# A spectral product whose VectorE half works in PSUM, small steps moved to GpSimd, a last output in halves, and new instruction orders

## Chip, cores and metric
The kernel runs on one core of one Trainium2 chip. The metric is the device time in microseconds of one execution; several executions give a median. Engines are called PE (TensorE), DVE (VectorE), ACT (ScalarE), POOL (GpSimd) and SP (SyncE).

## What is computed
Four batches of 512 tokens x 128 features pass through two layers; a context of 77 rows x 96 features is attended to. Cut to its outline:
```
x                                     # (4, 512, 128)
layer 0:
  scores of 4 heads over 77 context rows; only the 32 largest of a row are kept, softmax over these
  FiLM: scale and shift of the normed x from the attended context (film_in)
  s4d:  K from 64 complex states per feature; Kf = rfft(K), xf = rfft(z); y = irfft(xf * Kf); + D_skip
  FiLM again (film_out), norm, FFN with gelu, norm (norm 2), gated residual
  FFN whose two weights are butterfly products of 9 stages (512 wide)
layer 1:
  attention of 16 heads, 8 wide, over the 77 rows, gated residual
  mixture of 8 experts, rank 32, top 2: (silu(x Wu) * x Wv * gate) Wo, gated residual
```

## The kernel before, in words
Everything stays on chip: one batch is a tile of 128 partitions x 4 x 128. Each engine works through a hand-written list of steps, `ORDER` (lines 71 to 143): a step is a name and a batch, `mixr/0` for example, and an engine starts nothing of a later step before it has issued the earlier one. Between engines stand semaphores with constant values. `BANKS` (187 to 212) gives each PE step its PSUM banks, of which there are 8 of 128 x 512 floats; `readers` (399) says whose end makes a bank free. The steps of batch b + 1 are woven into those of batch b.

The steps that the change and the prediction touch:

- Attention of layer 0, for each batch and tile of 128 tokens: `score` (PE), four `round`s on DVE (line 1189: 4 times the 8 largest of a row, then replaced), `pick` (POOL, 1603), `wsum` and `winv` (DVE), `weigh` (POOL, 1608), `attnT` (PE). There are 64 rounds.
- Weight preparation: names that begin with `s_`. `s_ufly`, `s_udense`, `s_dfly`, `s_dhigh`, `s_dlow` (POOL) build the butterfly weights, `s_t1`, `s_wup`, `s_bup`, `s_t2`, `s_wdn`, `s_cwup` multiply them on PE, `s_pc`, `s_qc`, `s_kern`, `s_freq` give the spectrum of the state kernel, `s_misc` (DVE, 1470) scales two weights and fills two pads.
- The spectral part of a batch: `film_in` (PE, DVE 1234), `dft` on PE (two banks, even and odd tokens, 570), ACT copies the even bank to `XF` (942), DVE `dft` (1242) forms sum and difference with the odd bank, both in `XF`. Then `mixr` and `mixi` (DVE 1253, POOL 1617) multiply with `H0f` and `H1f`, the real and the imaginary part of the product, nine instructions each. DVE has `mixr` of batches 0, 1 and 3, POOL `mixr/2` and all four `mixi`. `idft` on PE waits for both. `film_pre` (PE, ACT, POOL 1556) prepares the second FiLM, `film_out` and `film_add` (DVE 1275) apply it, `stat1`, `rs1`, `norm1` and `lift1` follow.
- The first FFN: `ffn_up` (PE, ACT), `ffn_down` (PE, DVE 1285), then `stat2`, `rs2`, `norm2` (DVE, 1163), `gain` and `x1` (POOL), `stat3`, `norm3`, `lift3` and the second FFN, `fold_up` and `fold_down`.
- Attention of layer 1: `q`, `scoreA` (PE; DVE takes the maxima, 1172), `maxT` (DVE, 1177: the maximum as three bf16 terms in four dependent instructions; then PE, then ACT), `keyA`, `mixA`, `normA`, `wo`.
- The experts: `lift5`, `logits`, `top2` (DVE), `units` (PE, silu on ACT, product on DVE), `gate0` and `gate1` (POOL, 1573, two tiles each), `turn0` and `turn1` (four transposes each on PE, 678, a copy each on ACT), `moe_out` (PE; DVE adds, 1339). SP sends a batch's output (480) when it is added.

The elementwise helpers have one line each: L1118 is DVE's `tensor_tensor`, L1496 POOL's, L837 ACT's activation, L499 PE's matmul. `chain` issues an instruction and waits for it, `linked` only marks it. Setting up DMAs is SP's work alone. The code puts the two halves of the product so:
```
linked(tt(m0, x[:, :, 0, :, :], both(H0f[:, i, :, :]), ALU.mult))
chain(tt(m1, x[:, :, 1, :, :], both(H0f[:, 1 - i, :, :]), ALU.mult))
chain(tt(out, m0, m1, ALU.add if i else ALU.subtract))
```
where `x` is `XF` in SBUF.

## Time and profile before
| | us |
|---|---|
| median of 3 runs (334.46 to 335.09) | 334.61 |
| the profiled execution, its own time | 336.93 |
| its span, first to last instruction | 335.10 |
| PE busy in the span | 258.3 (77%) |
| DVE busy | 261.9 (78%) |
| ACT busy | 226.1 (67%) |
| POOL busy | 188.6 (56%) |

A profile is one execution, and its span lies inside its own time. Busy shares are means over stages that differ. The granted TensorE clock was 0.903 of full speed over the span. A row of a group gives its busy time, the mean of one instruction, and the idle time of the engine just before it with what ended it. A chain is followed back from the last instruction through what released each step.

### The profile page before, as it was taken

Reading aid. Unit: us, or ns where it says so; the run is one execution under the profiler, and the core shown is the slowest. Engines: PE = TensorE matmul, PEld = TensorE weight load, DVE = VectorE, ACT = ScalarE, POOL = GpSimd, SP = SyncE. Lnnn points to the kernel's source line nnn. Section 1 sums busy time; section 2 is a strip of 40 time slices with the busy share of each in tenths; the row PEclk is TensorE's granted clock in tenths of the full one; section 3 lists DMA queues with packets and bytes.
Section 4 is the critical chain, followed back from the end, with each engine's and each line's share of the span. In section 5 each row is a group of like instructions: output and inputs, shape, how many; then the busy total and the mean of one; then the engine's idle time right before and its main releaser. Section 6 shows DMA issues by size and latency. Waiting matters only on the chain.

```text
...
## 1 busy us (share of the span) xinstructions
PE 258.3 (77%) x1778; PEld 162.7 (49%) x1778; DVE 261.9 (78%) x1354; ACT 226.1 (67%) x534; POOL 188.6 (56%) x268
## 2 busy tenths in 40 slices
...
DMA packets 4663, 10.28 MB, mean 31 GB/s; under 512 B 659, under 2 KB 2836, under 8 KB 4374
## 3 DMA queue, kind: packets, MB, share of 16 engines
...
q8 instruction: 14, 0.23, 0.3%
...
## 4 chain that ended last, share of the span: by engine, by line
PE 47%; DVE 17%; POOL 15%; ACT 10%; issue 6%; POOLq 0%; ACTq 0%; DVEq 0%
PE bank L499 43%; ACT arena L837 5%; POOL arena L1496 5%; POOL MT L1496 4%; DVE arena L1118 4%; DVE R L1216 3%; DVE V L1204 2%; PE bank L521 2%; POOL k0bd L1496 1%; DVE KT L1447 1%; POOL bt L1496 1%; POOL sel L1606 1%; PE bank L683 1%; ACT E L837 1%; DVE st L1150 1%
## 5 line engine op out<-in xcount | busy, mean ns | idle before, releaser
L837 ACT ACTIVATE arena<-bank 128x512 f32<-128x512 f32 (+2 forms) x63 | 32.8, 597 | 21.2 <-PE bank L499 14.3
L1216 DVE MATCH_REPLACE8 R<-V,R 128x77 f32<-128x77 f32 x192 | 40.6, 223 | 0.0
L831 ACT ACT_TABLE_LOAD x29 | 37.2, 1283 | 4.2 <-DMA pack_kgen<-in_kgen 3.7
L1496 POOL TENSOR_TENSOR pack_bfly<-pack_bfly,bt 128x512 f32<-128x512 f32 x8 | 8.2, 1048 | 52.4 <-DVE bt L1118 42.7
L499 PE MATMUL bank<-arena 128*32 128x16 f32 (+3 forms) x304 | 13.2, 223 | 30.9 <-DVE arena L1118 29.6
L1204 DVE MAX8 V<-R 128x8 f32<-128x77 f32 x192 | 31.1, 224 | 0.4
L1174 DVE TENSOR_REDUCE bt<-bank 128x4 f32<-128x308 f32 x64 | 25.8, 468 | 5.8 <-PE bank L499 5.7
L499 PEld LDWEIGHTS bank<-arena 128*32 128x32 f32 (+1 forms) x304 | 9.9, 143 | 36.4 <-DVE arena L1118 31.2
L837 ACT ACTIVATE E<-bank,negm,rs 128x77 f32<-128x77 f32 x64 | 21.3, 415 | 7.3 <-POOL sel L1496 5.3
L499 PE MATMUL bank<-pack_bfly,arena 32*128 32x512 f32 (+3 forms) x136 | 21.0, 528 | 1.0 <-ACT pack_bfly L837 0.7
L1496 POOL TENSOR_TENSOR k0bd<-sel,w 128x308 f32<-128x308 f32 x16 | 11.6, 727 | 15.3 <-ACT w L837 15.0
L499 PE MATMUL bank<-pack_moe,LO 128*128 128x512 f32 (+1 forms) x64 | 19.6, 432 | 0.8 <-DVE bt L1174 0.5
L499 PE MATMUL bank<-LO,pack_ffn 128*128 128x512 f32 x32 | 17.8, 706 | 0.7 <-ACT LO L837 0.7
L499 PE MATMUL bank<-VW,AT 78*128 78x128 f32 x128 | 16.1, 279 | 2.4 <-ACT pack_dft L837 0.9
L1606 POOL TENSOR_SCALAR sel<-R 128x308 f32<-128x308 f32 x16 | 16.0, 1001 | 3.2 <-issue 2.2
L837 ACT ACTIVATE arena<-MT 128x128 f32<-128x128 f32 x74 | 17.3, 428 | 0.5 <-DVE MT L1118 0.5
L499 PEld LDWEIGHTS bank<-VW,AT 78*128 78x128 f32 x128 | 15.0, 192 | 4.3 <-ACT AT L837 2.0
L499 PE MATMUL bank<-arena,pack_dft 128*128 128x256 f32 x48 | 14.5, 447 | 2.5 <-DVE arena L1118 2.5
L1496 POOL TENSOR_TENSOR XG<-XG,pack_rows 128x512 f32<-128x512 f32 x4 | 5.1, 1272 | 18.9 <-DVE XG L1123 18.9
L499 PEld LDWEIGHTS bank<-pack_dft,arena 128*128 128x128 f32 x128 | 14.9, 192 | 1.1 <-issue 1.0
L1216 DVE MATCH_VALUE_LOAD R<-V,R 128x8 f32 x192 | 15.2, 79 | 0.4 <-POOL sel L1496 0.4
L499 PEld LDWEIGHTS bank<-pack_ffn,arena 128*128 128x128 f32 x128 | 14.9, 192 | 0.8 <-ACT arena L837 0.7
...
## 6 DMA issues: line engine op xcount, KB each, us to landing
...
```

The lines of the kernel that those rows point to most:

```text
L499: return nc.tensor.matmul(out, lhsT, rhs, start=start, stop=stop, **kw)
L521: last = nc.tensor.transpose(o[:, P * t:P * t + P], src[:, b, t, :], I)
L683: last = nc.tensor.transpose(o[:, P * t:P * t + P], SUT[:, t, P * tile:P * tile + P], I)
L831: nc.scalar.add_instruction(mybir.InstLoadActFuncSet(name=nc.get_next_instruction_name(), act_func_set_id=need, ins=[], outs=[]))
L837: return nc.scalar.activation(out, in_, func, **kw)
L1118: return nc.vector.tensor_tensor(out, x, y, op)
L1150: linked(nc.vector.bn_stats(st6[:, n, t, :], src[:, b, t, :]))
L1174: nc.vector.tensor_reduce(mx1[:, b % 2, tile, r, :], bank(f"sA{tile}_{r}", b)[:, 0:FLAT] .rearrange("p (h k) -> p h k", h=HG), AX.X, ALU.max)\
L1204: top = nc.vector.max(V8[:, g % 2, h, r, :], src[h])
L1216: swap = nc.vector.match_replace(R8[:, g % 2, r % 2, h, :], V8[:, g % 2, h, r, :], src[h], NEG)
L1496: return nc.gpsimd.tensor_tensor(out, x, y, op)
L1606: chain(nc.gpsimd.tensor_scalar(sel[:, g % 2, :, :], R8[:, g % 2, 1, :, :], -1.0e38, None, ALU.is_le))
```

## The change
- The spectral product: ACT copies the even bank to the second half of `XF`. DVE's `dft` forms sum and difference in four 256-wide instructions and writes them to the PSUM banks `d0` (real) and `d1` (imaginary) themselves. A new ACT step `xf` copies both banks to `XF` for POOL, in every batch. DVE's `mixr` works on the banks in PSUM, in nine instructions; POOL's halves read `XF` as before, in a new layout, and wait for the second copy.
- `maxT`'s split, `norm2` of all batches and `s_misc` go from DVE to POOL.
- Batch 3's experts: `gate0` on POOL takes tiles 0 and 1 one by one, `gate1` on DVE tiles 2 and 3. `turn0` transposes tiles 0 and 1 for both banks, `turn1` tiles 2 and 3. One copy is ACT's, the other DVE's. `moe_out` and a new `moe_rest` take half the tokens each, and each half has its own transfer; there are five output transfers for four.
- All four orders and the bank numbers are new.

The diff, cut; of the orders the lines of which the text speaks:
```diff
     "pe": """
...
-        score1/2 s_bup idft/0 score2/2 film_out/0 score3/2 vw/1 lift1/0 ffn_up0/0 ffn_up1/0 score0/3 s_t2
-        ffn_down/0 attnT/1 film_in/1 dft/1 s_cwup s_wdn film_pre/1 lift3/0 vw/2 vw/3 fold_up0/0 fold_up1/0
...
-        mixA1/3 mixA2/3 moe_out/1 wo/3 turn0/2 lift5/3 turn1/2 logits/3 units0/3 units1/3 units2/3 units3/3
-        moe_out/2 turn0/3 turn1/3 moe_out/3
...
+        s_bup vw/2 score2/2 idft/0 film_out/0 s_wup score3/2 s_cw1 lift1/0 ffn_up0/0 ffn_up1/0 s_t2 ffn_down/0
+        attnT/1 film_pre/1 score0/3 film_in/1 vw/3 s_cwup dft/1 score1/3 k1/0 s_wdn lift3/0 fold_up0/0
...
+        units2/1 units3/1 lift4/3 wo/2 q/3 turn0/1 scoreA0/3 turn1/1 scoreA1/3 scoreA2/3 scoreA3/3 lift5/2
+        moe_out/1 logits/2 maxT/3 keyA0/3 keyA1/3 mixA0/3 keyA2/3 mixA1/3 mixA2/3 units0/2 units1/2 units2/2
+        wo/3 units3/2 lift5/3 logits/3 turn0/2 turn1/2 units0/3 units1/3 units2/3 units3/3 moe_out/2 normA/3
+        turn0/3 turn1/3 moe_out/3 moe_rest/3
...
     "dve": """
...
-        film_in/0 round3_1/1 wsum0/1 round0_3/1 dft/0 winv0/1 round1_2/1 round1_3/1 wsum1/1 winv1/1 round2_2/1
-        stat0/3 round3_2/1 round2_3/1 round3_3/1 mixr/0 round0_0/2 round1_0/2 wsum2/1 round0_1/2 round2_0/2
-        round3_0/2 winv2/1 film_out/0 s_bup film_add/0 stat1/0 round0_2/2 wsum3/1 round1_1/2 round2_1/2
...
+        winv0/1 winv1/1 dft/0 nmr0/1 round0_0/2 s_freq mixr/0 round1_0/2 wsum2/1 round0_1/2 round2_0/2
+        round3_0/2 winv2/1 round1_1/2 wsum3/1 round0_2/2 film_out/0 film_add/0 round2_1/2 stat1/0 wsum0/2
...
+        stat5/3 top2/3 units0/3 units1/3 units2/3 units3/3 gate1/3 moe_out/2 turn1/3 moe_out/3 moe_rest/3
     "pool": """
...
-        s_ufly2 s_ufly3 weigh1/0 pick3/0 s_ufly4 weigh2/0 weigh3/0 s_ufly5 s_ufly6 s_ufly7 pick0/1 s_ufly8
-        s_udense pick1/1 mixi/0 weigh0/1 pick2/1 s_dfly2 s_dfly3 s_dfly4 s_dfly5 weigh1/1 pick3/1 film_pre/0
...
+        s_ufly1 s_ufly2 s_dfly2 s_ufly3 s_ufly4 s_dfly3 s_dfly4 weigh2/0 weigh3/0 pick0/1 pick1/1 s_ufly5
+        s_ufly6 s_ufly7 s_ufly8 s_udense s_rows film_pre/0 weigh0/1 weigh1/1 pick2/1 mixi/0 pick3/1 weigh2/1
...
+        s_dfly5 pick0/2 s_dfly6 s_dfly7 s_dfly8 s_dhigh weigh3/1 pick1/2 x_bias/0 weigh0/2 pick2/2 norm2/0
+        gain/0 x1/0 s_dlow film_pre/1 weigh1/2 mixi/1 pick3/2 s_v1 weigh2/2 weigh3/2 x_bias/1 pick0/3 s_misc
+        pick1/3 k1/0 norm2/1 gain/1 x1/1 mixi/2 maxT/0 mixr/2 film_pre/2 k1/1 k1/2 weigh0/3 x_bias/2 pick2/3
...
+        def mixed(b, i):
+return [(s["dft_moved"], 3 * b + i)] + [made("mixr", b)] * (("mixr", b) in SCHEDULE["dve"])
...
-for b in range(B):
+for b in range(B - 1):
     sp.wait_ge(s["x4_ready"], b + 1)
     sp.dma_start(tokens(out_dram[b]), by_parity(X[:, b, :, :])).then_inc(stored, 16)
-sp.wait_ge(stored, 16 * B)
+for c in range(2):
+    sp.wait_ge(s["x4_ready"], B + c)
+    sp.dma_start(tokens(out_dram[B - 1])[:, c], by_parity(X[:, B - 1, :, :])[:, c]).then_inc(stored, 16)
+sp.wait_ge(stored, 16 * (B + 1))
...
+    elif step.startswith("turn") and b == B - 1:
+        if tile == 0:
+            pe.wait_ge(s["weighted"], 2 * b + 1)
+            claim("turn0", b)
+            claim("turn1", b)
+        else:
+            pe.wait_ge(s["gated"], NT * B + 1)
+        for j in range(2):
+            for t in (2 * tile, 2 * tile + 1):
+                last = nc.tensor.transpose(bank(f"turn{j}", b)[:, P * t:P * t + P], SUT[:, t, P * j:P * j + P], I)
+            if tile == 1:
+                last.then_inc(s["turn_ready"], 1)
     elif step.startswith("turn"):
...
+    elif step in ("moe_out", "moe_rest"):
+        o = claim("moe" if step == "moe_out" else "moe_rest", b)
         pe.wait_ge(s["turned"], 2 * b + 2)
-        for t in range(NT):
+        for t in (range(NT) if b < B - 1 else range(0, 2) if step == "moe_out" else range(2, NT)):
...
-        a(XF[:, 0, :, :, :].rearrange("p s c d -> p (s c d)"), bank("d0", b)[:, :], ACT.Copy).then_inc(s["dft_moved"], 1)
+        a(flat4(XF[:, 1, :, :, :]), bank("d0", b)[:, :], ACT.Copy).then_inc(s["dft_moved"], 1)
+    elif step == "xf":
+        for i in range(2):
+            act.wait_ge(s["dft_copied"], 4 * b + 2 * i + 2)
+            a(flat4(XF[:, i, :, :, :]), bank(f"d{i}", b)[:, :], ACT.Copy).then_inc(s["dft_moved"], 1)
...
-        dve.wait_ge(s["dft_moved"], b + 1)
-        low, high = (XF[:, f, :, :, :].rearrange("p s c d -> p (s c d)") for f in range(2))
-        tt(high, low, bank("d1", b)[:, :], ALU.subtract).then_inc(s["dft_copied"], 1)
-        tt(low, low, bank("d1", b)[:, :], ALU.add).then_inc(s["dft_copied"], 1)
+        dve.wait_ge(s["dft_moved"], 3 * b + 1)
+        even, odd = flat4(XF[:, 1, :, :, :]), bank("d1", b)
+        for i in range(2):
+            x, y, o = even[:, CH * i:CH * i + CH], odd[:, CH * i:CH * i + CH], bank(f"d{i}", b)
+            if i == 1:
+                dve.wait_ge(s["dft_copied"], 4 * b + 2)
+            tt(o[:, 0:CH], x, y, ALU.add).then_inc(s["dft_copied"], 1)
+            tt(o[:, CH:2 * CH], x, y, ALU.subtract).then_inc(s["dft_copied"], 1)
     elif step == "s_freq":
...
-    elif step in ("mixr", "mixi"):
-        dve.wait_ge(s["dft_copied"], 2 * b + 2)
+    elif step == "mixr":
+        dve.wait_ge(s["dft_copied"], 4 * b + 4)
         if b == 0:
             dve.wait_ge(s["freq_copied"], 3)
         if b >= 1:
             dve.wait_ge(s["y_ready"], b)
-        i, x = int(step == "mixi"), XF
+        re, im = (bank(f"d{i}", b)[:, :].rearrange("p (f c d) -> p f c d", f=2, c=2) for i in range(2))
         both = lambda t: t.unsqueeze(2).broadcast_to([P, 2, 2, D])
-        out = YZ[:, i, :, :, :]
-        m0, m1 = (MT[:, 2 * i + k, :, :].rearrange("p f (c d) -> p f c d", c=2) for k in range(2))
-        linked(tt(m0, x[:, :, 0, :, :], both(H0f[:, i, :, :]), ALU.mult))
-        chain(tt(m1, x[:, :, 1, :, :], both(H0f[:, 1 - i, :, :]), ALU.mult))
-        chain(tt(out, m0, m1, ALU.add if i else ALU.subtract))
-        linked(tt(m0[:, :, 0, :], x[:, :, i, 0, :], H1f[:, 1, :, :], ALU.mult))
-        chain(tt(m1[:, :, 0, :], x[:, :, 1 - i, 0, :], H1f[:, 0, :, :], ALU.mult))
-        chain(tt(out[:, :, 1, :], out[:, :, 1, :], m0[:, :, 0, :], ALU.add))
-        chain(tt(out[:, :, 1, :], out[:, :, 1, :], m1[:, :, 0, :], ALU.subtract if i else ALU.add))
-        low, high = (YZ[:, i, f, :, :].rearrange("p c d -> p (c d)") for f in range(2))
-        even, odd = halves(i)
+        out = YZ[:, 0, :, :, :]
+        k0, k1 = (MT[:, 0, k, :].rearrange("p (f d) -> p f d", f=2) for k in range(2))
+        m1 = MT[:, 1, :, :].rearrange("p f (c d) -> p f c d", c=2)
+        dve.wait_ge(s["dft_moved"], 3 * b + 2)
+        chain(tt(k0, re[:, :, 0, :], H1f[:, 1, :, :], ALU.mult))
+        linked(tt(re, re, both(H0f[:, 0, :, :]), ALU.mult))
+        dve.wait_ge(s["dft_moved"], 3 * b + 3)
+        linked(tt(k1, im[:, :, 0, :], H1f[:, 0, :, :], ALU.mult))
+        chain(tt(m1, im, both(H0f[:, 1, :, :]), ALU.mult))
+        chain(tt(re[:, :, 1, :], re[:, :, 1, :], k0, ALU.add))
+        chain(tt(re[:, :, 1, :], re[:, :, 1, :], k1, ALU.add))
+        chain(tt(out, re, m1, ALU.subtract))
+        low, high = (YZ[:, 0, f, :, :].rearrange("p c d -> p (c d)") for f in range(2))
+        even, odd = halves(0)
         tt(even, low, high, ALU.add)
...
+    elif step == "gate1":
+        dve.wait_ge(s["gated"], NT * b + NT)
+        dve.wait_ge(s["gate_ready"], b + 1)
+        x = SUT[:, 2:4, :].rearrange("p t (e r) -> p t e r", e=NE)
+        tt(x, x, W8[:, b % 2, 2:4, :].unsqueeze(3).broadcast_to([P, 2, NE, RE]), ALU.mult).then_inc(s["gated"], 1)
+    elif step == "turn1":
+        dve.wait_ge(s["turn_ready"], 2 * b + 2)
+        dve.wait_ge(s["moe_ready"], 2 + b)
+        nc.vector.tensor_copy(SU[:, 1, :], bank("turn1", b)[:, :]).then_inc(s["turned"], 1)
+    elif step in ("moe_out", "moe_rest") and b == B - 1:
+        half = int(step == "moe_rest")
+        dve.wait_ge(s["moe_ready"], 2 + b + 1 + half)
+        x, part2 = X[:, b, 2 * half:2 * half + 2, :], slice(256 * half, 256 * half + 256)
+        tt(flat(x), bank("moe_rest" if half else "moe", b)[:, part2], flat(x), ALU.add).then_inc(s["x4_ready"], 1)
...
+    elif step == "maxT":
+        hi, mid, lo = (MXS[:, :, :, HG * i:HG * i + HG] for i in range(SPLIT))
+        pool.wait_ge(s["maxed"], RG * NT * (b + 1))
+        if b == 0:
+            linked(nc.gpsimd.memset(MXS[:, :, :, :], 0.0))
+            pool.wait_ge(s["pool_link"], link[0])
+        if b >= 1:
+            pool.wait_ge(s["maxT_ready"], b)
+        chain(nc.gpsimd.tensor_copy(hi, mx1[:, b % 2, :, :, :]))
+        chain(tt(mxr[:, :, :, :], mx1[:, b % 2, :, :, :], hi, ALU.subtract))
+        chain(nc.gpsimd.tensor_copy(mid, mxr[:, :, :, :]))
+        tt(lo, mxr[:, :, :, :], mid, ALU.subtract).then_inc(s["split_ready"], 1)
...
+    elif step.startswith("gate") and b == B - 1:
+        pool.wait_ge(s["gate_ready"], b + 1)
+        for i in range(2):
+            pool.wait_ge(s["gated"], NT * b + i + 1)
+            x = SUT[:, i, :].rearrange("p (e r) -> p e r", e=NE)
+            last = tt(x, x, W8[:, b % 2, i, :].unsqueeze(2).broadcast_to([P, NE, RE]), ALU.mult)
+        last.then_inc(s["weighted"], 1)
...
-        pool.wait_ge(s["dft_copied"], 2 * b + 2)
+        pool.wait_ge(s["dft_moved"], 3 * b + 3)
```

## Rows read from the trace of the kernel before

**Rows 1.** Stretch, length; busy us of PE, PEld, DVE, ACT, POOL; clock; DMA share
```profile
20.00:110.00 90.00, 42.35 (x431) 30.56 (x432) 86.61 (x530) 58.86 (x174) 81.15 (x130) 0.70 0.07 25
...
145.00:327.20 182.20, 175.62 (x1157) 104.56 (x1155) 126.95 (x576) 130.56 (x267) 72.48 (x89) 1.00 0.01 4
327.20:335.10 7.90, 3.12 (x24) 2.72 (x24) 1.38 (x2) 1.08 (x2) 0.61 (x1) 1.00 0.19 66
```

**Rows 2.** Stretches again, of instructions on tile MT alone (DVE's spectral products)
```profile
93.20:99.40 6.20, 0.00 (x0) 0.00 (x0) 5.50 (x8) 0.00 (x0) 0.00 (x0) 0.70 0.00 0
147.50:152.40 4.90, 0.00 (x0) 0.00 (x0) 4.41 (x8) 0.00 (x0) 0.00 (x0) 1.00 0.02 5
232.20:237.30 5.10, 0.00 (x0) 0.00 (x0) 4.54 (x8) 0.00 (x0) 0.00 (x0) 1.00 0.00 2
```

**Rows 3.** DVE instructions on tile MT: min/median/max ns, first and last start
```profile
L1118 DVE TENSOR_TENSOR MT<-arena,pack_film x6: 677/930/1227, 93.2 to 233.3; 128x512 f32<-128x512 f32 x6
```

**Rows 4.** Groups by form on DVE: busy us, mean ns, idle before
```profile
L1118 DVE TENSOR_TENSOR pack_bfly<-bank,pack_bfly 128x256 f32<-128x256 f32 x16 | 5.9, 418 | 1.5 <-ACT pack_bfly L837 1.5
...
L1118 DVE TENSOR_TENSOR arena<-arena,bank 128x512 f32<-128x512 f32 x8 | 5.1, 675 | 0.8 <-PE bank L499 0.8
...
L1118 DVE TENSOR_TENSOR XG<-HN,XG 128x512 f32<-128x512 f32 x4 | 2.8, 690 | 0.1
```

**Rows 5.** Groups by form on ACT
```profile
L837 ACT ACTIVATE arena<-bank 128x512 f32<-128x512 f32 x45 | 23.9, 610 | 14.9 <-PE bank L499 8.1 <-PE bank L683 6.7
```

**Rows 6.** Groups by form on POOL
```profile
L1496 POOL TENSOR_TENSOR bt<-pack_bfly,v 128x64 f32<-128x64 f32 x6 | 3.0, 521 | 0.2
...
L1553 POOL TENSOR_SCALAR HN<-X,rs 128x128 f32<-128x128 f32 x4 | 2.3, 603 | 17.8 <-ACT rs L837 17.8
...
L1496 POOL TENSOR_TENSOR bt<-pack_bfly,bflyh 128x64 f32<-128x64 f32 x6 | 1.9, 336 | 0.2
```

**Rows 7.** Groups by form on DVE: norm 2, and two of the split's four
```profile
L1123 DVE TENSOR_SCALAR XG<-XG,mv,rs 128x128 f32<-128x128 f32 x16 | 5.0, 373 | 0.3 <-ACT rs L837 0.3
...
L1118 DVE TENSOR_TENSOR pack_bfly<-pack_bfly 128x64 bf16<-128x64 f32 x4 | 1.5, 368 | 0.1
...
L1186 DVE CAST pack_bfly<-bt 128x64 bf16<-128x64 f32 x4 | 0.9, 229 | 0.1
```

**Rows 8.** The chain that ended last, in order of time: start us, us, what
```profile
40.02 0.56 DVE V L1204 x4
40.58 0.83 DVE R L1216 x4
...
114.70 6.71 PE bank L499 x8
```

**Rows 9.** Timeline: start us, us, instruction, in brackets the idle time before it
```profile
84.96 1.27 POOL L1496 TENSOR_TENSOR MT<-arena,pack_film 128x512 f32<-128x512 f32 x1
...
103.04 1.43 PE L499 MATMUL bank<-MT,pack_dft 128*128 128x256 f32 x4
...
108.82 0.69 DVE L1118 TENSOR_TENSOR HN<-bank,AO 128x512 f32<-128x512 f32 x1 [1.72 <-POOL XG L1496]
```

**Rows 10.** Timeline of PE, the two waits for DVE's maxima
```profile
295.15 0.63 PE L683 MATMUL bank<-pack_first,pack_bfly 128*128 128x128 f32 x4 [0.71 <-DVE bt L1174]
...
301.04 1.95 PE L499 MATMUL bank<-pack_moe,LO 128*128 128x512 f32 x4 [0.54 <-DVE bt L1174]
```

**Rows 11.** Timeline of the tail
```profile
325.76 2.05 POOL L1496 TENSOR_TENSOR pack_bfly<-pack_bfly,bt 128x512 f32<-128x512 f32 x2 [8.98 <-DVE pack_bfly L1118]
...
329.79 2.02 PE L499 MATMUL bank<-pack_moe,arena 128*128 128x128 f32 x16 [0.83 <-ACT arena L837]
331.85 0.69 DVE L1118 TENSOR_TENSOR X<-bank,X 128x512 f32<-128x512 f32 x1 [3.93 <-PE bank L499]
```

**Rows 12.** Timeline of POOL, the first step of two weighs
```profile
93.34 1.15 POOL L1496 TENSOR_TENSOR k0bd<-sel,w 128x308 f32<-128x308 f32 x1
...
103.86 0.70 POOL L1496 TENSOR_TENSOR k0bd<-sel,w 128x308 f32<-128x308 f32 x1
```

194 lines of the change are left out of this document (88 added, 106 removed).

## The prediction
> **What bounds the kernel now.** I read the busy time by stretch first, then the chain of waits, then groups and single rows. The stretches [rows 1] show two regimes. From 20 to 110 us VectorE (DVE) is busy 86.6 of 90 us and GpSimd (POOL) 81.2, while TensorE (PE) has 42.4 and runs at a mean granted clock of 0.70 (1.0 is 2.4 GHz, 0.5 is 1.2): attention's top-32 rounds and the weight preparation set the pace. From 145 to 327.2 us PE is busy 175.6 of 182.2 us at full clock, so only 6.6 us there are PE's idle time, and DVE has 55 us free. Between them lies a ramp, and after 327.2 a serial tail of 7.9 us with 3.1 us of matmuls. So time can come from four places: an earlier end of the first regime, PE work placed ahead of the ramp's end, PE's 6.6 us, and the tail. A share of busy time on DVE after 145 is worth nothing by itself.
>
> The profiled execution took 336.93 us around a span of 335.10; the median of the runs is 334.61, 2.3 below it. I make the sum as a difference against that execution and take it off the median.
>
> **Part by part.**
>
> *Spectral product.* DVE runs three of these (b = 0, 1, 3; `mixr/2` is GpSimd's). Eight of the nine instructions took 5.50, 4.41 and 4.54 us [rows 2]; with the ninth (a 256-wide one, 0.45) a product is 5.3 on average. The dear ones read two SBUF operands: 677 ns at best, 1227 at worst for the same 512 columns [rows 3]. New: three 512-wide at the price of a form with one PSUM input, 0.68, and six 256-wide at 0.42 [rows 4], together 4.6. That saves 0.7 three times. `dft` becomes four 256-wide (1.68) for two 512-wide (1.35), 0.3 dearer four times. DVE nets 0.9 us. No row shows DVE writing PSUM: for 512 columns the ends are 0.60 (the ACT row that reads a bank [rows 5], less for a write that doesn't leave PSUM) and 0.93 (the median of the SBUF form), and I take 0.68, the row whose read side is the same; the ends are 3 x 3 x -0.08 = -0.7 us and 3 x 3 x 0.25 = +2.2. ScalarE (ACT) gets two more copies of 0.61 [rows 5] in each of four batches, 4.9 us, hidden by its 52 idle us in the PE-bound stretch. For GpSimd they are latency: it starts after the second copy, about 1.0 us later than the old pair of 0.675.
>
> The rows give 512 columns 0.68 with a PSUM input and 0.69 with two SBUF inputs [rows 4]. The Trainium skill, page "VectorE: DVE Perf Modes", section on the TRN2 errata, charges 120 cycles a VectorE instruction from PSUM against 58 from SBUF. By that rule, an estimate from the page, three products (27 instructions of 65 ns more) would be about 1.7 us dearer, wiping out the gain, and the median 332.7, inside the first case's spread. This trace doesn't show such a difference, so the sum goes by the rows.
>
> *Norm 2 to GpSimd.* DVE loses 5.0 us [rows 7]. The nearest GpSimd row is 0.60 for 128 columns with one scalar [rows 6], 2.4 us a batch; with two scalars perhaps up to 1.0 each, 4.0. I take 2.4. Latency per batch is +1.0 against DVE's 1.25, and at b = 0 DVE no longer does `film_in/1` first, so it is even there. Behind it wait `gain` and `x1` of the same queue.
>
> *Maxima's split.* On DVE four instructions between 0.23 and 0.37 [rows 7], about 1.3 us a batch; on GpSimd 64-column rows are 0.34 to 0.52 [rows 6], so 1.6 to 2.4. I take 1.9: 0.6 later into `maxT`, with PE steps (fold_down or logits) put before it. At b = 0 it stands between `mixi/2` and `mixr/2`, and its wait for the last maximum blocks the latter. `s_misc`: 0.9 us off DVE, about 1.6 on, in a GpSimd queue that has room then.
>
> *First regime.* A round is 0.56 + 0.83 us plus its joints, 1.45 [rows 8]. Ahead of DVE's `film_out/0` the new order has two more rounds (2.9), `wsum3/1` (0.5) and the dearer `dft/0` (0.3), less `mixr/0`'s 1.4 (6.0 there) and 0.4 of small steps: 1.9 more. But `film_out/0` waited 1.72 for GpSimd's `film_pre/0` [rows 9], which now runs before `mixi/0`. So it starts at 109.0 instead of 108.8. Ahead of `mixi/0` GpSimd gets s_dfly2 to 4 (3.7), `film_pre/0` (1.3), two weighs (2.9) and a pick (1.8), 9.7 us, less some 3 us of waits it had: 85.0 + 6.7 = 91.7, at the latest 97. It ends 8.4 later (84.96 to the next step's 93.34 before [rows 9, 12]) at 100 to 105.4; idft takes 3.1, so y is there at 103.2 to 108.5, under DVE's 109.0. The old idft started at 103.0 [rows 9], behind s_wup and s_bup on PE. By `ffn_down/0` DVE's work ahead is equal (0.2 apart), and `ffn_up`, 6.7 us of PE at the low clock, sets it [rows 8]. I take 0, from -3 (full clock there, no DVE waits) to +3.
>
> *Ramp.* Ahead of `fold_up0/0` PE has now also done score1/3 (0.8) and k1/0 (0.3): -1.1. Film_pre/1 now precedes mixi/1, so film_out/1 no longer waits 0.4: -0.4.
>
> *PE-bound stretch.* PE's work is unchanged. Of its 6.6 idle us, DVE's maxima made 1.25 in two waits [rows 10]; DVE has 11.5 us less before the tail. But scoreA1 to A3 of b = 3 now stand together, so PE will wait for maxima there (6.5 of DVE for 3.2 of PE), repaid by lift5/2, moe_out/1 and logits/2 covering the split. I take -1.0, from -4 to +3.
>
> *Tail.* Before [rows 11]: GpSimd's two gates to 327.81, transposes to 328.96, two ACT copies, then 2.02 of matmuls from 329.79, add 0.69, transfer. New: DVE gates tiles 2 and 3 while GpSimd does 0 and 1, ready about 327.2, when PE ends `moe_out/2`. Transposes to 328.4, copies on ACT and DVE side by side to 329.1, matmuls to 331.1, the last add 0.42 to 331.6 against 332.54. The first half's transfer is under it. -1.0, and 0.1 for half the bytes: -1.1. A DMA issue more on the otherwise empty SP queue costs nothing on the path.
>
> Sum: 0 - 1.1 - 0.4 - 1.0 - 1.1 = -3.6, so 336.93 becomes 333.3 for that execution, and the median 331.0.
>
> **Rivals.**
> *The first regime really shortens* (0.20). DVE's work up to the end of attention is about 4.3 us less (two norms, the first split, the products); if its waits also go and PE finds full clock earlier, the ramp starts 3 to 4 sooner: 331.0 - 3.5 = 327.5. For: DVE's 96% before 110. Against: at `ffn_down/0` the work ahead hasn't changed.
> *GpSimd becomes the bound* (0.24), the slow side. Its place is `mixi/0`: 9.7 us pulled ahead of it on an engine already busy 90% [rows 1]. It decides once mixi/0 ends after about 106. With contended prices (that stretch has 1.15 for a weigh's first step against 0.70 [rows 12]) and 3 us waiting for the last pick it ends at 109.5, y at 112.6, 3.6 late; norm 2 at its upper price adds 1.6 at b = 0, the split 0.5. The later gains are then worth 2.5 less the 1.0 that DVE no longer frees: 334.6 + 3.6 + 1.6 + 0.5 - 3.5 = about 336.8.
> *Only the tail counts* (0.14). The PE-bound stretch absorbs the rest: 334.61 - 1.1 = 333.5, or 334.4 if one of the new joints costs 1.0.
> The forecast's own case has 0.42, spread 329 to 333.
>
> **Numbers.** About 0.2% (0.67 us) is what a measurement can tell from no change. Faster: 0.42 + 0.20 + a little under half of 0.14 = 0.68; same 0.08; slower 0.24. The range takes in 327.5 less 1.7 and the slow case's 336.8: 325.8 to 336.8.
>
> **What would show it.** Right: `film_out/0` without a wait for GpSimd near 109; DVE's product instructions at 0.68 and 0.42, with no spread, DVE busy some 250 us and GpSimd 204; `fold_up0/0` within 1 us of 145; PE idle 5 to 6 us from there to moe_out/2; from the last GpSimd gate to the end 7 us. Wrong: DVE's `film_out/0` or PE's idft waiting for GpSimd by over 2 us, 128-column norms of 1 us on GpSimd, PSUM-writing instructions above 0.8, PE idle above 9 us after the ramp, or the low clock lasting beyond 145.

## The result, and the profile of the changed kernel

The changed kernel takes 341.46 us, the median of three runs (340.56 to 349.93); the kernel before 334.61. The ratio is 1.0172, with a 95% interval from 1.0144 to 1.0201: slower by 5.8 us by the ratio, where I had forecast 331.0. Two later sets of runs, on other chips, gave 1.0174 (1.0033 to 1.0315) and 1.0136 (1.0091 to 1.0180), 5.8 and 4.6 us. Kernels here fall at times into a slower state, of which the 349.93 is one execution; ratios, intervals and spans leave such executions out, and where the profiled one was of them (the changed kernel's first, its second repetition, "norm 2 back", "product back") nothing rests on TensorE's time in it alone. What follows is read from a second profile of the changed kernel, 339.78 us around a span of 338.0.

The busy time by stretch of that execution (columns as in [rows 1]):

```profile
20.00:110.00 90.00, 40.01 (x425) 29.72 (x426) 88.87 (x550) 54.29 (x170) 78.06 (x130) 0.70 0.08 28
110.00:145.00 35.00, 30.61 (x164) 21.11 (x164) 32.12 (x190) 26.77 (x64) 30.88 (x43) 1.00 0.01 2
145.00:331.60 186.60, 177.28 (x1148) 105.49 (x1147) 117.24 (x542) 129.49 (x264) 87.46 (x121) 0.98 0.01 4
331.60:338.00 6.40, 2.93 (x25) 2.53 (x23) 2.23 (x4) 0.60 (x1) 0.00 (x0) 1.00 0.23 82
```

The ramp (second row) has its full clock now, and the tail (fourth) is 6.4 us where it was 7.9 [rows 1]. But the PE-bound stretch went from 182.2 to 186.6 us: PE's idle time in it grew from 6.6 to 9.3, and its busy time by 1.7, though the matmuls are the same and nearly 4 us of them now stand before 145 (`fold_up0/0` starts 2.6 us earlier, with 1.1 us of steps put ahead of it). Its mean granted clock is no longer full (0.98; 1.0 is 2.4 GHz, 0.5 is 1.2). PE's timeline shows the place (start us, us, instruction, in brackets the idle time before it and what ended it):

```profile
174.44 1.36 PE L507 MATMUL bank<-arena,pack_bfly 32*128 32x308 f32 x8
178.12 1.18 PE L507 MATMUL bank<-arena,pack_bfly 32*128 32x308 f32 x8 [2.33 <-DVE bt L1200]
179.24 0.82 PE L529 MATMUL bank<-pack_first,HN 128*128 128x128 f32 x4
179.99 3.73 PE L507 MATMUL bank<-arena,pack_bfly 32*128 32x308 f32 x16
183.65 5.06 PE L507 MATMUL bank<-LO,pack_dft 128*128 128x512 f32 x8
```

These are `scoreA0/0`, `scoreA1/0`, `lift3/1`, `scoreA2/0` with `scoreA3/0`, and `fold_up` of batch 1. (A matmul in f32 stands as two instructions, so x8 is four matmuls, and `fold_up0/1` is the first half of the last row.) PE waits for DVE's maxima, and then `fold_up0/1` takes 3.35 us instead of 1.98. In the kernel before PE came to these steps later, did not wait, and ran all of `fold_up` in 3.70 us:

```profile
177.01 2.47 PE L499 MATMUL bank<-arena,pack_bfly 32*128 32x308 f32 x16
182.74 3.70 PE L499 MATMUL bank<-LO,pack_dft 128*128 128x512 f32 x8
178.07 1.40 DVE L1174 TENSOR_REDUCE bt<-bank 128x4 f32<-128x308 f32 x3
```

The same stretch of the changed kernel by windows, with the clock in the third column from the end:

```profile
174.00:178.00 4.00, 1.79 (x13) 0.91 (x11) 2.52 (x13) 2.69 (x8) 3.92 (x4) 1.00 0.00 0
178.00:181.00 3.00, 2.88 (x20) 2.04 (x23) 2.09 (x6) 1.71 (x5) 2.84 (x4) 0.77 0.00 0
181.00:188.00 7.00, 7.00 (x22) 3.24 (x15) 6.59 (x36) 2.42 (x4) 5.94 (x12) 0.61 0.01 2
```

Four microseconds with PE busy 1.79, then ten at a mean clock of 0.66, so 6.8 of them at 1.2 GHz.

The orders differ too much to compare step by step. So I put every matmul to its step (by count, against the order list), took for each kind of step the shortest time it has in any trace, and compared the moments at which equally much of this work was left. In us against the profiled execution of the kernel before (minus is ahead):

```
work left, near       changed  tail   norm 2   product  two-matmul  norm+round  norm+banks+round
                               alone  alone    alone    filler      (t11)       (t7)
175  ffn_down/0        -2.5    -0.6    -1.4     -0.6      -2.2       -2.7        -2.2
135  film_pre/2        -2.4    -0.7    +0.4     +1.1      -1.4       -2.7        -1.4
125  keyA1/0           +2.3    -0.7    +5.3     +2.6      +0.6       -2.1        -1.4
 90  lift3/2           +3.3    -0.7    +7.3     +4.3      +1.6       -0.4        +0.4
 70  logits/0          +2.0    -0.7    +6.9     +3.5      +0.3       -2.4        -1.7
 50  mixA0/2           +4.4    -0.7    +7.0     +3.5      +2.7       +3.2        +0.8
  5  units3/3          +4.4    -0.6   +10.2     +1.7      +2.7       +4.5        +0.4
  0  moe_out/3         +2.7    -2.4   +10.2     +1.7      +1.0       +2.7        -1.3
```

The change is 2.5 us ahead at the end of the first regime, loses 4.7 within 10 us of work at the first batch's maximum scores, 2.4 more in batch 2 (between 70 and 50), and gains 1.7 in the tail. From its first row to the one before the last it goes from -2.5 to +4.4. The execution compared is among the changed kernel's better ones: its spans are 337.8 to 341.9 us, at granted clocks of 0.87 to 0.91, where the kernel before has 0.90 to 0.91 in most of its runs. And the profiled execution of before is 1.4 to 2.3 us above the medians of its sets (336.93 against 335.54 and 334.61). So the two profiles differ by 2.9 us, where the medians of the second repetition differ by 5, and the table shows only part of the loss.

### The profile page after: what moved, and what is told of

Read it like the earlier page. It is cut to its first block, busy times and chain, and to the rows that moved or that the text cites. A ratio compares the mean times of both kernels' runs of the same rounds, so it can differ in the third digit from the quotient of the medians.

```text
span 348.1 us, 6239 instructions
## 1 busy us (share of the span) xinstructions
PE 272.4 (78%) x1778; PEld 171.2 (49%) x1778; DVE 255.2 (73%) x1328; ACT 226.8 (65%) x539; POOL 203.1 (58%) x305
## 4 chain that ended last, share of the span: by engine, by line
PE 46%; DVE 14%; ACT 5%; POOL 5%; issue 2%; POOLq 0%; DVEq 0%; ACTq 0%
PE bank L507 43%; DVE R L1229 4%; ACT arena L858 3%; DVE V L1217 3%; POOL XG L1575 2%; DVE bt L1200 2%; PE bank L529 1%; DVE bank L1144 1%; DVE arena L1144 1%; ACT pack_bfly L858 1%; DVE MT L1144 1%; DVE st L1176 1%; ACT LO L858 1%; POOL X L1521 1%; POOL XG L1521 1%
## 5 line engine op out<-in xcount | busy, mean ns | idle before, releaser
L858 ACT ACTIVATE arena<-bank 128x512 f32<-128x512 f32 (+2 forms) x70 | 36.6, 600 | 15.5 <-PE bank L507 10.1
L507 PE MATMUL bank<-arena 128*32 128x16 f32 (+3 forms) x304 | 17.1, 239 | 9.0 <-DVE arena L1144 6.9
L507 PE MATMUL bank<-arena,pack_bfly 32*128 32x308 f32 x128 | 19.5, 523 | 4.9 <-DVE bt L1200 4.1
L1521 POOL TENSOR_TENSOR pack_bfly<-pack_bfly,bt 128x512 f32<-128x512 f32 (+1 forms) x8 | 7.5, 940 | 23.6 <-DVE pack_bfly L1144 23.6
L507 PEld LDWEIGHTS bank<-arena 128*32 128x32 f32 (+1 forms) x304 | 13.4, 165 | 15.0 <-issue 7.6
L1144 DVE TENSOR_TENSOR X<-bank,X 128x512 f32<-128x512 f32 (+1 forms) x13 | 8.4, 646 | 15.5 <-PE bank L507 15.4
L1144 DVE TENSOR_TENSOR pack_bfly<-bank,pack_bfly 128x256 f32<-128x256 f32 (+1 forms) x20 | 9.0, 476 | 14.6 <-ACT pack_bfly L858 14.6
L858 ACT ACTIVATE LO<-bank 128x512 f32<-128x512 f32 x16 | 9.5, 598 | 15.5 <-PE bank L529 15.4
L507 PE MATMUL bank<-LO,pack_dft 128*128 128x512 f32 x32 | 17.0, 676 | 1.4 <-ACT LO L858 1.4
L1575 POOL TENSOR_SCALAR XG<-XG,mv,rs 128x128 f32<-128x128 f32 x16 | 12.5, 793 | 8.9 <-ACT rs L858 8.8
```

The lines of the kernel that those rows point to most:

```text
L507: return nc.tensor.matmul(out, lhsT, rhs, start=start, stop=stop, **kw)
L858: return nc.scalar.activation(out, in_, func, **kw)
L1144: return nc.vector.tensor_tensor(out, x, y, op)
L1521: return nc.gpsimd.tensor_tensor(out, x, y, op)
L1575: last = nc.gpsimd.tensor_scalar(dst[:, b, t, :], src[:, b, t, :], mv[:, tile, b, t, 0:1], rs[:, tile, b, t:t + 1], ALU.subtract, ALU.mult)
```

## The experiments

*The changed kernel again.* First, once more alone; then on the chip of the next three kernels.

> The changed kernel once more, unchanged, because its first profiled run was a disturbed one. Theory 1 (the clock: TensorE has less work in small pieces before 50 us, stands for 2 to 4 us at some new joints and then runs the next tens of matmuls at 1.2 GHz, late in the kernel too) expects 341 us within 1, a mean granted clock of 0.88 to 0.89 against 0.903 before, VectorE, ScalarE and GpSimd no busier than in the kernel before, and at least two stretches at the low clock behind 145 us that the kernel before does not have. Theory 2 (the GpSimd queue became the bound) expects the clock after 145 us to be full as before, and the idle time of TensorE to grow by 6 us or more, put down to GpSimd. Theory 3 (the first regime only ends later) expects fold_up of the first batch to start at 150 us or later instead of 145, and everything behind it as far apart as before.

> The changed kernel unchanged, on the chip of the next three, so that they can be set against it on one chip: 340 to 342 us, ratio to before 1.015 to 1.02.

339.78 us at best, clock 0.909 in the profile; GpSimd's work after 145 has grown (87.5 us for 72.5), but of PE's waits after 142 none is put down to it. Theory 3 falls: `fold_up0/0` starts at 142.40. Theory 1 has the mechanism, but not its size: one stretch at the low clock behind 145 in this profile, not two. The 6.8 us at half clock are worth at most 3.4 us of work, and PE's idle time has grown by 2.7, so both count, and about equally. Theory 2 falls by its own test, though not in substance, as the DVE row below shows. The second set: 340.56.

*Other banks.*
```diff
- scoreA1/0:7350 lift3/1:1 scoreA2/0:6573 scoreA3/0:0145
+ scoreA1/0:6451 lift3/1:0 scoreA2/0:7346 scoreA3/0:5170
```
(left out: other banks for `fold_up` of batch 1 too, and 1 and 5 exchanged from `fold_down/1` on)

> The changed kernel with other PSUM banks for the four maximum-score steps of the first batch (scoreA1 to A3) and what follows them; no order and no instruction is changed. Theory A (the loss sits where the scores for the row maxima stand: scoreA1/0's first bank is one whose maximum VectorE takes third, so TensorE waits 2.33 us and then runs the next 7 us of matmuls at the low clock) expects scoreA1/0 to start within 0.3 us of scoreA0/0's end, fold_up of batch 1 to start 2 to 3 us earlier and to take 1.98 instead of 3.35 us, and the undisturbed executions 3 to 4 us shorter, 336 to 337 us against 339.8. Theory B (VectorE's sixteen maxima, 6.5 us, set that place whatever the banks) expects less than 1 us. Theory C (the loss comes from the parts moved to GpSimd) expects nothing, within 0.3 us.

Ratio 1.0277 (1.0239 to 1.0316), slower than the changed kernel. `scoreA1/0` started at once, and the wait came back one and two steps later; PE began `fold_up0/1` at 183.25, 0.4 us earlier than in the changed kernel, and at the low clock (whole, the last row is 6.15 us for x8):

```profile
175.56 2.32 PE L507 MATMUL bank<-arena,pack_bfly 32*128 32x308 f32 x14
178.47 0.78 PE L507 MATMUL bank<-arena,pack_bfly 32*128 32x308 f32 x2 [0.59 <-DVE bt L1200]
179.98 0.66 PE L529 MATMUL bank<-pack_first,HN 128*128 128x128 f32 x4 [0.73 <-DVE bt L1200]
180.57 2.75 PE L507 MATMUL bank<-arena,pack_bfly 32*128 32x308 f32 x16
183.25 4.64 PE L507 MATMUL bank<-LO,pack_dft 128*128 128x512 f32 x5
```

So these banks are not the bound at this place (theory A falls, B stands for it): sixteen maxima of 0.47 us are, from the moment DVE can start them. That the whole is some 4 us slower than the changed kernel, no theory expected.

*The parts alone, in the old orders.* The tail:
```diff
- units3/3 moe_out/2 moe_out/3
+ units3/3 gate1/3 moe_out/2 turn1/3 moe_out/3 moe_rest/3
```
(left out: the code of gates, transposes, and halves of the sum and of the output)

> The kernel before, its orders and banks untouched, with the tail part of the change alone: the last batch's gates on both engines, its second copy of the transposes on VectorE, the last product, sum and output in halves. My prediction's price was 1.1 us; the changed kernel's undisturbed trace has 6.4 us from the end of moe_out/2 to the end of the span, where the kernel before had 7.9. Theory A expects 1.1 to 1.5 us less than the kernel before, 335.4 to 335.8 for an execution like the profiled one of before (336.93). If the saving needs the new orders around it, 0.5 or less.

333.73 us against 335.51, ratio 0.9949 (0.9929 to 0.9969): by its interval the only kernel of all that beats the one before, and so the version to keep. The table gives it 1.7 us between 5 us before the end and the end.

All small moves (norm 2, the split, the small set-up step), and norm 2 alone, which in outline is:
```diff
- norm2/b (VectorE)     gain/b (GpSimd)
+                       norm2/b gain/b (GpSimd)
```

> The kernel before with the small moves alone, in the old orders: norm 2 of every batch, the maxima's split and the small set-up step go from VectorE to GpSimd, at the nearest place in its queue. Theory A (the new orders and banks lose the time, not the moves) expects within 1 us of the kernel before either way. Theory C (GpSimd's slower norm, 3.1 us a batch against 1.1 on VectorE, and a split of 1.6 ahead of maxT are on the path) expects 2 to 5 us more, with TensorE waiting for GpSimd at fold_up or maxT of several batches.

> The kernel before with norm 2 alone moved to GpSimd, directly ahead of gain in its queue; nothing else. With all small moves the old orders lost some 14 us. If the norm is the cause (3.13 us a batch against 1.11 on VectorE, all of it ahead of gain, x1 and stat3), batch 0 loses about 2 us at fold_up0/0 and batch 1 about 2 at the maximum scores, and with the low clock behind such waits it is 4 to 12 us. If the maxima's split is the cause, this run is within 2 us of before.

Ratios 1.0446 (1.0374 to 1.0518) and 1.0332 (1.0304 to 1.0360). Theory A was wrong about the moves, C right in sign and far too low (all of them cost 15 us): norm 2 alone costs 11 here. Its price (group by form, in the changed kernel's profile; columns as in [rows 6, 7]):

```profile
L1575 POOL TENSOR_SCALAR XG<-XG,mv,rs 128x128 f32<-128x128 f32 x16 | 12.5, 795 | 7.0 <-ACT rs L858 6.9
```

and the place, PE in the kernel before with norm 2 alone on GpSimd:

```profile
177.41 1.58 PE L498 MATMUL bank<-arena,pack_bfly 32*128 32x308 f32 x12
179.71 0.89 PE L498 MATMUL bank<-arena,pack_bfly 32*128 32x308 f32 x4 [0.72 <-DVE bt L1173]
...
182.27 3.36 PE L498 MATMUL bank<-arena,pack_bfly 32*128 32x308 f32 x16
185.56 6.21 PE L498 MATMUL bank<-LO,pack_dft 128*128 128x512 f32 x8
```

It is the place of the changed kernel, and again the clock falls behind it: `fold_up` takes 6.21 us for 3.70. Two more losses follow, in the maximum scores of batch 1 (+2.0) and the key scores of batch 3 (+3).

The product alone (old orders, the copies added, `scoreA3/1` put ahead of `units2/0`, banks chosen anew), and the reverse, the changed kernel with the product back in SBUF:
```diff
-                "d1": [(s["dft_copied"], 2 * b + 2)], "y": [(s["y_scaled"], b + 1)],
+                "down": [(x_ready["v"], b + 1)], "d0": mixed(b, 2), "d1": mixed(b, 3), "y": [(s["y_scaled"], b + 1)],
...
+                elif step == "xf":
```
(left out: the copies themselves; the two banks `d0` and `d1` are free only when ScalarE's copies and `mixr` are done)

> The kernel before with the spectral product's part alone (VectorE's half in PSUM, four butterflies, ScalarE's two extra copies), the old orders but for the new copies and one pair of TensorE steps swapped, and banks chosen anew for the longer hold of dft's two banks. VectorE saves 0.3 us a product less the dearer butterflies; the two banks are held 15 to 20 us in batches 0 and 3, in batch 3 through the maximum scores of batch 1, where nine banks would be wanted. Theory D (bank pressure) expects 2 to 4 us lost between 222 and 230 us and about that in all; my prediction's terms alone expect within 1 us of before.

> The changed kernel with the spectral product put back as it was (VectorE reads and writes SBUF, two butterflies, one ScalarE copy per batch instead of three), in the new orders and with the new banks. Theory A expects the wait at scoreA1/0 to stay, because its banks are the same, and the time within 1 us of the changed kernel. Theory D (the product in PSUM itself costs: two banks held until ScalarE's two extra copies are done, the copies ahead of film_pre's) expects 1.5 to 4 us less than the changed kernel, with the waits behind dft of each batch gone.

1.0116 (1.0080 to 1.0153) and 1.0594 (1.0522 to 1.0666). Alone the product costs 3.9 us by the ratio and 2.0 between the two profiled executions. That is theory D's sum, but only a part of it lies at the place D had named (222 to 230 us): 1.2 to 1.3 at `fold_down/0` to `idft/1`, 1.5 at batch 0's maximum scores and 1.1 around `units` of batch 0, where PE's `scoreA3/1` takes 1.88 us for 0.80 and `units3/0` waits 0.92. At the maximum scores the clock falls here too:

```profile
182.00:186.00 4.00, 4.00 (x22) 2.29 (x23) 2.13 (x7) 1.89 (x3) 3.77 (x5) 0.57 0.00 0
```

How much of the cost is the held banks, and how much the two extra copies or the new bank numbers elsewhere, no run separates. Taking it out of the new orders, though, costs some 15 us (1.0594 against 1.014 to 1.017), which no theory expected. DVE's instructions on the product's tile in that kernel (min/median/max ns, first and last start):

```profile
L1134 DVE TENSOR_TENSOR MT<-arena,pack_film x6: 680/767/1754, 93.2 to 245.1; 128x512 f32<-128x512 f32 x6
L1134 DVE TENSOR_TENSOR MT<-arena,pack_kgen x6: 837/1159/1487, 95.7 to 248.8; 128x256 f32<-128x256 f32 x6
```

the second of these groups in the kernel before, where GpSimd's half ran at another time:

```profile
L1118 DVE TENSOR_TENSOR MT<-arena,pack_kgen x6: 416/424/653, 95.9 to 235.1; 128x256 f32<-128x256 f32 x6
```

and the same multiplications in PSUM, in the changed kernel:

```profile
L1144 DVE TENSOR_TENSOR MT<-bank,pack_kgen x6: 410/414/424, 93.7 to 234.6; 128x256 f32<-128x256 f32 x6
L1144 DVE TENSOR_TENSOR bank<-bank,MT x6: 432/432/433, 95.8 to 236.1; 128x256 f32<-128x256 f32 x6
L1144 DVE TENSOR_TENSOR bank<-bank,pack_film x3: 699/699/699, 94.1 to 234.0; 128x512 f32<-128x512 f32 x3
```

The new orders run `mixr/0` (93.7 to 99.7) beside GpSimd's `mixi/0` (95.5 to 104.1); the old ones had them one behind the other [rows 2, 9, 12]. With SBUF operands and GpSimd beside it a 256-column multiplication takes 837 to 1487 ns, with an operand in PSUM at most 424; `mixr/0` takes 9.3 us against 6.0. So the product in PSUM is what makes the overlap of the two engines cheap. How the 15 us come out of that was not followed step by step.

*Norm 2 back on VectorE, in the new orders*, in outline:
```diff
- (GpSimd) norm2/b gain/b
+ (GpSimd) gain/b   (VectorE) round3_3/2 norm2/0 · film_in/2 norm2/1 · scoreA2/1 norm2/2 · wo/1 norm2/3
```

> The changed kernel with norm 2 of all four batches back on VectorE and nothing else. Theory N (the norm on GpSimd costs 3.13 us a batch where VectorE took 1.1, and in batches 0 and 1 all of it is latency of the chain norm 2, gain, x1, stat3: VectorE waits 1.68 and 1.48 us for x1 just before stat3) expects stat3 1.5 to 2 us earlier in batch 0 and 0.7 to 1 in batch 1, fold_up of batch 0 to start near 140.5 instead of 142.4, and 2 to 4 us less in all, 336 to 338. Theory B (VectorE's queue ahead of the sixteen maxima sets the pace, and the norm only fills it again) expects fold_up0/0 earlier but scoreA3/0 where it was, and less than 1 us in all. A loss of more than 1 us would say that VectorE is the bound there.

Inconclusive by its time: one execution of four counts, 339.16. But `fold_up0/0` was no earlier in it (142.79, against 142.40), and in t11 and t7 below, which have norm 2 back too, it starts at 142.19 and 142.74: at batch 0 ScalarE gets to the copy of `lift3/0` only at 142.1 (t7), behind the product's two extra copies, `s_cwup` and `k1/0`. Here theory N is wrong.

*Useless work in the wait.* Four, then two matmuls of `fold_up`'s shape behind `scoreA0/0`, into a free bank that nobody reads:
```diff
- scoreA0/0 scoreA1/0
+ scoreA0/0 spare/0 scoreA1/0
```

> The changed kernel with four useless matmuls of 512 columns (about 2 us at the full clock) behind scoreA0/0, in the 2.33 us in which TensorE waits for VectorE's maxima; they write a free PSUM bank that nobody reads. Theory C (the wait costs twice: itself, and then 6.8 us of the low clock over fold_up of batch 1) expects the clock to stay full there, fold_up0/1 to take 1.98 instead of 3.35 us, and the undisturbed executions 1.5 to 3.5 us shorter although work was added. Without that mechanism: the same time as the changed kernel, or up to 0.5 us more.

> The changed kernel with two useless matmuls of 512 columns behind scoreA0/0; one takes about 0.95 us, so they fill 1.9 of the 2.33 us for which TensorE waits there. If the low clock behind the wait is worth what the trace says (fold_up0/1 3.35 instead of 1.98 us, and some 0.4 us in the small steps), the clock stays full to the end and the time is 1.5 to 2 us below the changed kernel's, 338 to 338.7, with 3 us of the 5 lost at this place left. If the clock falls anyway, 340 as without.

Four took 3.63 us, not the 2 I had reckoned, and gave 1.0130 (1.0088 to 1.0171); two gave 1.0102 (1.0039 to 1.0165), a median of 338.06 us where the changed kernel had 340.56 on another chip. The intervals of both overlap the changed kernel's (1.0091 to 1.0180), so the whole time doesn't tell; the trace does, at this place. PE with the two, and its windows:

```profile
176.76 1.98 PE L507 MATMUL bank<-LO,pack_ffn 128*128 128x512 f32 x4
179.16 1.18 PE L507 MATMUL bank<-arena,pack_bfly 32*128 32x308 f32 x8 [0.42 <-DVE bt L1204]
...
180.86 2.56 PE L507 MATMUL bank<-arena,pack_bfly 32*128 32x308 f32 x16
183.35 2.84 PE L507 MATMUL bank<-LO,pack_dft 128*128 128x512 f32 x6
```

```profile
175.00:178.00 3.00, 3.00 (x16) 1.63 (x16) 1.53 (x11) 1.76 (x4) 2.92 (x4) 1.00 0.00 0
178.00:181.00 3.00, 2.58 (x15) 1.16 (x14) 2.51 (x7) 1.82 (x7) 2.84 (x4) 1.00 0.00 0
181.00:188.00 7.00, 6.95 (x34) 3.80 (x35) 6.94 (x35) 4.80 (x7) 6.47 (x12) 1.00 0.01 2
```

(Whole, the last row of the timeline is 3.70 us for x8.) Full clock over the place, and a loss of 2.0 us there (-1.4 to +0.6) instead of 4.7. Both PE and DVE come to it 1.03 us later in this execution (scores from 175.47, maxima from 177.89), whose clock was low from 143.7 to 147.1, so the two losses start from the same distance between the engines. So more than half of what the wait costs here is the clock behind it: nothing but useless work was added. The Trainium skill, page "TensorE: Matmul & The Clock Gate", section "What's actually happening", has this rule (the array's clock halves after idleness, and the same kernel may meet it differently from run to run). The traces agree with both: the clock fell behind the wait and not behind the filled one, and executions of the one changed kernel have mean clocks from 0.87 to 0.91. A fall that no wait explains comes below, in t11.

*Which edits carry the repair.* All three (t7: norm 2 back, other banks, one top-32 round from before to behind the maxima), then without the banks (t11), then without norm 2 (t12). The round's edit:
```diff
- film_in/2 norm2/1 round2_2/3 dft/2 ... scoreA3/0 round0_3/3
+ film_in/2 norm2/1 dft/2 ... scoreA3/0 round2_2/3 round0_3/3
```

> Norm 2 back on VectorE, the renamed banks of the earlier run, and one top-32 round (1.47 us) moved from before to behind the first batch's sixteen maxima on VectorE. Theory B (VectorE's place for the maxima is what TensorE waits for) expects scoreA0/0 on VectorE at 174.5 to 175.5 instead of 176.9, TensorE without a wait over 0.5 us among the maximum scores, fold_up0/1 begun by 181 at the full clock, and 4 to 6 us less than the changed kernel, 334 to 336. If the clock falls anyway, 2 us less.

> The changed kernel with norm 2 on VectorE and the one top-32 round behind the sixteen maxima, its PSUM banks as they are. If VectorE's start of the maxima carries the gain (they start 1 us or more earlier against the scores), the time is 335 to 337, with scoreA1/0's wait at most 1.3 instead of 2.33 us. If the banks are needed too, 338 to 341 and the low clock still follows the wait.

> The changed kernel with the renamed banks and the one round behind the maxima, norm 2 still on GpSimd. VectorE then stands 3 us before stat3/1, waiting for x1 behind GpSimd's norm, so the maxima can't start earlier: if norm 2's latency is the cause, the time stays at 340 to 344 and GpSimd's x1/1 is what stat3/1 waits for. If it isn't, 335 to 337 as with all three.

In this order the ratios are 1.0003 (0.9980 to 1.0026), 1.0270 (1.0189 to 1.0351) and 1.0254 (1.0214 to 1.0294). DVE before the maxima in the changed kernel:

```profile
172.76 1.56 DVE L1144 TENSOR_TENSOR bank<-arena,bank 128x256 f32<-128x256 f32 x4 [0.69 <-PE bank L507]
175.79 0.87 DVE L1176 BATCH_NORM_STATS2 st<-X 128x6 f32<-128x128 f32 x4 [1.48 <-POOL X L1521]
```

GpSimd in front of it:

```profile
169.92 3.13 POOL L1575 TENSOR_SCALAR XG<-XG,mv,rs 128x128 f32<-128x128 f32 x4 [0.81 <-ACT rs L858]
173.13 1.28 POOL L1521 TENSOR_TENSOR XG<-XG,pack_rows 128x512 f32<-128x512 f32 x1
174.49 1.27 POOL L1521 TENSOR_TENSOR X<-XG,X 128x512 f32<-128x512 f32 x1
```

and without norm 2 back, the round moved (t12): the wait is still there, so the maxima can't start earlier; with it back (t7) it is gone:

```profile
177.48 0.87 DVE L1175 BATCH_NORM_STATS2 st<-X 128x6 f32<-128x128 f32 x4 [1.47 <-POOL X L1520]
```
```profile
175.46 0.87 DVE L1173 BATCH_NORM_STATS2 st<-X 128x6 f32<-128x128 f32 x4
176.52 2.76 DVE L1197 TENSOR_REDUCE bt<-bank 128x4 f32<-128x308 f32 x7
```

(In t7 the maxima start at 176.52, not at 174.5 to 175.5 as expected, because PE's scores themselves came 1.0 us later, and PE waited 0.93 for ScalarE's norm before `lift3/1`.) Norm 2 with the round is what repairs this place: t11, with the old banks, passes it at -2.1 (table). Its maxima start at 175.19 instead of 176.86, and its PE waits 0.97 us instead of 2.33, with `fold_up` at the full clock:

```profile
176.47 1.18 PE L504 MATMUL bank<-arena,pack_bfly 32*128 32x308 f32 x8 [0.97 <-DVE bt L1197]
```

Whether norm 2 back would do there without the round, no run decides. That t11 is nonetheless no faster than the changed kernel is a second matter: its clock fell at 268 and again at 302 us, and t7's did not, though from 190 us on the two differ in the numbers of two banks only. The windows of t11, then those of t7 0.7 us later, at the same steps:

```profile
266.00:269.00 3.00, 2.87 (x24) 1.61 (x20) 2.02 (x4) 2.92 (x6) 1.91 (x2) 0.88 0.00 0
269.00:276.00 7.00, 7.00 (x37) 1.76 (x33) 2.58 (x18) 2.42 (x6) 0.00 (x0) 0.57 0.00 1
```
```profile
266.70:269.70 3.00, 2.87 (x28) 1.42 (x21) 1.99 (x4) 2.95 (x7) 1.94 (x2) 1.00 0.00 0
269.70:276.70 7.00, 7.00 (x65) 2.16 (x57) 2.79 (x20) 3.69 (x10) 0.00 (x0) 1.00 0.00 1
```

What decides it is open: PE is as busy in both just before, and has the same waits, so this fall isn't that of the place at 179 us, where PE had stood. t11's three spans are 338.0 to 341.2 us, t7's seven 332.9 to 334.6, so without the banks the repair of the place brings nothing in the whole, and why the banks matter is not shown.

*All remaining waits at once*, by orders and banks, on top of t7 (t8; left out here: `lift5/2` among batch 3's maximum scores, `mixr/1` one round later, the banks from batch 2's key scores on):
```diff
- scoreA1/0 lift3/1 scoreA2/0     idft/1 film_out/1 score2/3     keyA1/2 logits/1 keyA2/2 mixA0/2     norm3/0 xf/1 s_cwup k1/0 lift3/0
+ scoreA1/0 scoreA2/0 lift3/1     score2/3 idft/1 film_out/1     keyA1/2 mixA0/2 logits/1 keyA2/2     norm3/0 s_cwup lift3/0 xf/1 k1/0
```

> The kernel of the last run (norm 2 on VectorE, renamed banks, one round behind the maxima) with its remaining waits taken on, by orders and banks alone: in batch 0 ScalarE copies lift3 before the product's two extra copies; scoreA2/0 stands ahead of lift3/1; one text score stands ahead of idft/1; in batch 2 mixA0 stands between the key scores, and lift5/2 among batch 3's maximum scores. Theory B (what is lost behind the ramp are places where TensorE is ahead and finds a bank, a copy or a maximum not ready) expects fold_up0/0's wait 0.7 instead of 1.4 us, 0.5 us less at scoreA of batch 0, 0.5 to 1 less in batch 2 and 0.5 in batch 3: 332.5 to 334 where the last had 335.6. If it is 335 or more, the waits only move on.

335.56 us, ratio 1.0010 (0.9984 to 1.0036): a miss. Each wait it took away came back a step later (0.7 us won at `fold_up0/0`, 1.04 lost at `idft/1`, which then stood behind the later copies; 1.1 lost at `lift3/3`, 0.9 at `maxT/3`).

## Why the prediction was wrong, by its steps

*First regime and ramp: right in kind, low.* I had 0 and -1.5 (ramp's 1.1 and 0.4); the trace has -2.5 at `ffn_down/0` and a start of `fold_up0/0` 2.6 earlier, 142.40, outside the 1 us around 145 that I had named. `film_out/0` starts at 109.00 without a wait, as forecast; `mixi/0` runs from 95.5 to 104.1, inside the 91.7 to 97 and 100 to 105.4. GpSimd is busy 203.4 us (204), DVE 255.2 (250).

*The product: seven of its nine terms right, its gain absent, what it is for missed.* With an operand in PSUM 512 columns take 0.70, 0.68 and 0.69 us and 256 take 0.41 to 0.43, where I took 0.68 and 0.42. But the last two instructions of a product still read two SBUF operands, and GpSimd's half now runs beside them. Their group in the kernel before and in the changed one, and the very last of the changed `mixr/0` (0.55 us before):

```profile
L1118 DVE TENSOR_TENSOR MT<-arena x3: 425/425/443, 98.4 to 236.5; 128x256 f32<-128x256 f32 x3
L1144 DVE TENSOR_TENSOR MT<-arena x3: 515/843/856, 97.5 to 237.3; 128x256 f32<-128x256 f32 x3
98.23 1.48 DVE L1144 TENSOR_TENSOR arena<-arena 128x256 f32<-128x256 f32 x1
```

So a product takes 5.9, 5.0 and 5.3 us of DVE (b = 0, 1, 3) where I summed 4.6 and the kernel before has 6.0, 4.8 and 4.9: the 0.7 saved three times did not come. And I read the spread of the SBUF form [rows 3] as a price, and did not ask what stood beside it: GpSimd. The Trainium skill, page "SBUF — State Buffer", section "Who interferes with whom", says that a VectorE instruction with two SBUF inputs contends with a GpSimd instruction that reads SBUF; the rows of the product-back kernel agree (837 to 1487 ns against 414 and 432), and so do these. And I did not count the two banks that it holds, nor what the copies delay: alone, the part costs 2 to 4 us. The Trainium skill's rule that I did weigh, 120 cycles against 58 (page "VectorE: DVE Perf Modes", section on the TRN2 errata), isn't seen: PSUM to PSUM takes 699 ns and SBUF to SBUF 690 [rows 4].

*Norm 2: mis-sized, and its queue priced at nothing.* I took 0.60 a step, 2.4 a batch, from a form with one scalar; the form with two is 0.795, 3.13 a batch, under my upper bound of 1.0. I wrote that `gain` and `x1` wait behind it and charged nothing for that in batches 1 to 3. In batch 1 `x1` comes at 175.76, DVE's `stat3/1` waits 1.48 us for it at the head of DVE's queue, and behind `stat3/1` stand the sixteen maxima that PE's scores wait for.

*The PE-bound stretch is the step that failed.* I took -1.0 (from -4 to +3); between the table's -2.5 and +4.4 it is +6.9. I looked for the risk at `scoreA` of batch 3, where four steps now stand together; there the trace loses under 1 us. It loses 4.7 us of the 6.9 at `scoreA` of batch 0. I had summed PE's earlier arrival as a gain to keep. But an engine that comes 2.4 us earlier to a place where DVE is only 1.2 earlier (maxima from 176.86 instead of 178.07) waits, and the orders had taken `k1/3` and `score3/3` away from there, its cover. And I had reckoned the clock as full after 145, because before it was: "the low clock lasting beyond 145" stands among my signs of error, with no price in the sum. The wait of 2.33 us is worth about 5 with what follows it, and PE's idle time reached the "above 9 us" that I had named as a sign of error (9.3).

*The tail: right, low.* It gave -1.5 to -1.7 for -1.1 (from `moe_out/2`'s end to the span's end 6.4 us, 7.9 before; from the last GpSimd gate's end 7.2, where I had 7).

*Rivals.* "GpSimd becomes the bound" had the sign, less than half the size (+2.2 us), and the wrong place. Its sum also takes off 3.5 us where its own words leave the later gains 2.5 at most, so it should have ended at 337.8 or above. `mixi/0` was in time, and its term for norm 2 at the upper price (1.6 at batch 0) belonged to batch 1. "Faster" fell with the stretch above: by the table, without it the forecast was near (-2.4 and the tail's -1.7), though partly by luck, since the ramp gave 1 us more than I had summed and the product nothing.

*What stays open.* Batch 2 loses 2.4 us between `logits/0` and `mixA0/2`. The new order takes `moe_out/0` (2 us) out of its key scores, where ScalarE's 2.04 us a chunk meets PE's 1.36; that this is the cause is only argued, putting it back was not tried. Why the clock falls in t11 and not in its near twin t7 is open too, and so is the part of the loss that the medians show beyond the profiles (5 against 2.9 us).
